# A fused Mamba-2 and mixture-of-experts layer: activation tiles of the second loop's first two steps loaded ahead of the wait for the last scatter-add, first step's norms behind the shared layer

## Chip, cores and metric

The kernel runs on one core of one Trainium2 chip. The time is that of one execution on the device, in microseconds, as the median of three runs. PE is the matmul engine (TensorE; PEld are its weight loads), DVE the vector engine, ACT the scalar engine, POOL GpSimd, SP the sync engine, which issues most of the plain DMAs. Each engine works through its own list of instructions in order; semaphores tie the lists together.

## What is computed

```python
# x: [2, 4096, 256]
x = x + layernorm(mamba2(layernorm(x)))        # attention half, the kernel's first part
h = layernorm(x)
# feed-forward half, 8192 tokens, 64 experts, 8 per token, 128 slots for each expert
gu = h @ shared_gate_up_w                       # shared layer, inner width 512
shared = silu(gu[:, :512]) * gu[:, 512:] @ shared_down_w
shared = shared * sigmoid(h @ shared_gate_w)
probs = softmax(h @ gate_w); w, idx = top_k(probs, 8)
buf[e, slot] = h[token]                         # gather per expert, capacity 128
out_e = (silu(buf @ Wg) * (buf @ Wu)) @ Wd      # per expert, inner width 128
routed = sum over the token's experts of w * out_e
x = x + layernorm(routed + shared)
```

## The kernel before, in words

The first part (Mamba-2) leaves the residual x in SBUF (x_all), the normed and transposed activations in DRAM as 32 tiles (xnt_d, one tile is 2 x 128 tokens, 256 KB), the tables of token numbers for each expert, and zeros in routed_sum in DRAM. The part at issue has two software-pipelined loops over tiles and experts. A function iteration(i) is written for each engine; it is unrolled for the first four steps and the last ones and runs as a hardware loop for the middle. real(j, n) tells whether stage j exists in this step; follows(i) is false only in the very first step, i = 0.

**First loop** (iteration_r1, 16 steps). Each step takes four of the 64 experts: POOL gathers their tokens by indirect DMA, PE multiplies, ACT and DVE make silu and product, ACT scales the result into out_e, and POOL adds it to routed_sum in DRAM by an indirect DMA that adds (scatter-add). These scatter-adds are strictly one after another: each waits for the semaphore of the one before (added00, added01, added10, added11). Beside this each step computes the shared layer of one tile (tiles 0 to 15): ACT rounds the tile to xt_hi, DVE makes the rest xt_lo = xt - xt_hi and raises xt_split, PE does the up product in three passes for each of four column groups (up_shared, 12 matmuls each of 128x256) and the down product (down_shared, 12 matmuls for each batch), and the result is kept in SBUF (shared).

**Second loop** (iteration_r2, 8 steps, two trailing stages). Each step computes the shared layer of two more tiles (16 + 2 j in xt[0], 17 + 2 j in xt[1]) and finishes four tiles: two from the first loop's stored rows (indices 1 and 3 of routed, f_sum, f_norm) and two fresh ones (indices 0 and 2). To finish a tile means: load its rows of routed_sum (routed), add the shared part (f_sum), bn_stats, bn_aggr, on POOL the variance plus epsilon and the power -0.5, on DVE the shift, on ACT the norm (f_norm), on POOL the add to x_all (f_ready), on SP the store. The tiles routed, f_sum and f_norm lie in the same SBUF as the experts' buffers (out_e among them), xt does not.

The order of the lists, for step i = j0:

- SP (L1279 to L1317): in step 0 a wait for all scatter-adds (added11 at 256, L1283); loads routed[1] (L1285), xt[0] (L1288), xt[1] (L1291), routed[3] (L1294); the stores of earlier tiles and the load of routed[2] (L1309); wait for f_ready1, its store (L1313), load of routed[0] (L1316).
- PE (L1429 on): second half of the down product of the step before; wait for m_act_split3; two down products of the step before (bank 0); wait for xt_split; eight up_shared; first half of the down product of this step.
- ACT (L1552 on): m_act_high0 and m_act_high3 of the step before; f_norm[0] of two steps before; xt_hi[0], xt_hi[1]; f_norm[2] of two steps before; four silu and copies of the first tile, with f_norm[1] after the fourth silu (L1597); those of the second tile; at the end f_norm[3] (L1625).
- DVE (L1746 on): m_act_s 3, splits 0 and 3 of the step before (L1762, L1765, raises m_act_split3); f_sum[0] of the step before; add of routed[1] (L1780); xt_lo[0] (L1783, raises xt_split); statistics of f_sum[1] (L1792, L1798); add of routed[3] (L1802); xt_lo[1] (L1805); products and splits of both tiles, with the remaining steps of the norms between them (L1812, L1824, L1834, L1877).
- POOL (L1967 on): powers and adds; for step 0 variance 1 and power 1 (L1994, L1997), add of f_norm[1] (L2001), variance 3 and power 3 (L2004, L2007), and in step 1 the add of f_norm[3] (L1982).

Of the kernel before, what the change touches and what calls it, by code (L numbers as in the profile page):

```python
# [54 lines left out]
def plain(v):  # L55

    return v.bitcast(F32)
# [7 lines left out]
def build(nc, x_d, w_in_d, conv_w_d, conv_b_d, dt_bias_d, a_log_d, d_d, norm_w_d, w_out_d,  # L65
# [7 lines left out]
    with ctx:  # L73
# [1124 lines left out]
        m_xt_high = sem("m_xt_high")  # L1198
        m_gate_ready = sem("m_gate_ready")
# [28 lines left out]
        with nc.Block() as block:  # L1228
            @block.sync
            def _(eng):  # L1230
# [47 lines left out]

                def iteration_r2(i):  # L1279
                    j0, j1, j2 = i, i - 1, i - 2  # L1280
                    if real(j0, 8):
                        if is_number(j0) and j0 == 0:
                            eng.wait_ge(added11, 256)  # L1283
                        eng.nop(nofuse=True)
                        eng.dma_start(routed[:, 1], tokens_of(routed_d[0:TOK, :], 2 * j0 + 0)).then_inc(routed_loaded1, 16)  # L1285
                    if real(j0, 8):
                        eng.nop(nofuse=True)
                        eng.dma_start(xt[:, 0].rearrange("p k t -> p (k t)"), xnt_d[bass.ds(2 * j0 + 16, 1), :, :].rearrange("o p f -> (o p) f")).then_inc(xt_loaded, 16)  # L1288
                    if real(j0, 8):
                        eng.nop(nofuse=True)  # L1290
                        eng.dma_start(xt[:, 1].rearrange("p k t -> p (k t)"), xnt_d[bass.ds(2 * j0 + 17, 1), :, :].rearrange("o p f -> (o p) f")).then_inc(m_xt_loaded, 16)  # L1291
# [174 lines left out]
            def _(eng):  # L1466
# [85 lines left out]
                def iteration_r2(i):  # L1552
# [77 lines left out]
            def _(eng):  # L1630
# [115 lines left out]
                def iteration_r2(i):  # L1746
# [42 lines left out]
                    if real(j0, 8):  # L1789
# [4 lines left out]
                    if real(j0, 8):  # L1794
# [5 lines left out]
                    if real(j0, 8):  # L1800
# [8 lines left out]
                    if real(j0, 8):  # L1809
# [10 lines left out]
                    if real(j0, 8):  # L1820
# [11 lines left out]
                    if real(j0, 8):  # L1832
# [42 lines left out]
                    if real(j0, 8):  # L1875
# [8 lines left out]
                    if real(j1, 8):  # L1884
# [4 lines left out]
                        last.then_inc(f_stats2, 1)  # L1889
                pipeline(eng, iteration_r2, 4, 8, 10)  # L1890
# [152 lines left out]
```

## Time and profile before

| | |
|---|---|
| runs | 1491.86, 1495.43, 1496.35 us |
| median | 1495.43 us |
| span of the profiled execution | 1491.0 us, from its first to its last instruction |
| its own time | not given apart; only the three times above |
| PE busy | 1259.5 us (84%) |
| DVE busy | 1054.9 us (71%) |
| ACT busy | 937.5 us (63%) |
| POOL busy | 845.2 us (57%) |
| mean granted TensorE clock | 0.947 |

A row of an engine in order of time has the start in the span, the duration, the engine, the line of the kernel, the operation, out<-in by the program's names and the shapes, and in brackets the idle time of the engine before it with what ended it. experts_arena is the SBUF region that holds xt, routed, f_sum, f_norm and the small norm tiles, counts holds silu_s and act_s, bank is PSUM. L1468 is the line of a copy helper on ACT. The clock is given as a share of full speed: 1.0 is 2.4 GHz, 0.5 is 1.2 GHz.

### The profile page before, as it was taken

The page shows a single profiled execution, that of the slowest core. Times are in us where ns is not written, and L with a number is a line of the kernel's source. Part 1 is how long each engine was busy: PE and PEld are TensorE (multiplying, and loading weights), DVE is VectorE, ACT ScalarE, POOL GpSimd, SP SyncE. Part 2 cuts the span into 40 slices and gives each one's busy share as a digit, 9 for nine tenths or more (in the row PEclk, how much of TensorE's full clock was granted, in tenths as well). Part 3 has the DMA queues.
Part 4 walks back from the last instruction along what each step waited for, and adds up shares of the span by engine and source line. Part 5 has one row for each costly group of instructions (what it writes and reads, how often), then busy time and mean ns, then how long its engine had stood idle before and what let it go on. Part 6 is the DMA issues. An engine that isn't in the chain of part 4 may idle for free. (4 is left out here: it accounts for less than half of the span.)

```text
span 1491.0 us, 27525 instructions
## 1 busy us (share of the span) xinstructions
PE 1259.5 (84%) x8578; PEld 1095.7 (73%) x8578; DVE 1054.9 (71%) x3152; ACT 937.5 (63%) x2097; POOL 845.2 (57%) x1039
## 2 busy tenths in 40 slices
PE   2898999999999999999999998268877888749995
PEld 2677787787787787787787786268777887739995
DVE  3788899899899899899899896423233333328995
ACT  2777877877877878878878876623333333325663
POOL 0365566566566565565565565156766667624554
PEclk9999999999999999999999999579899989979998
DMA  5500110010010010010010000466666666624452
GB/s 165 171 15 15 33 39 24 32 37 23 32 37 23 32 37 23 32 37 23 32 37 23 21 29 19 119 181 161 148 156 155 164 152 161 136 46 132 153 159 94
DMA packets 110628, 115.66 MB, mean 78 GB/s; under 512 B 19633, under 2 KB 98801, under 8 KB 110577
## 3 DMA queue, kind: packets, MB, share of 16 engines
q1 hardware_dynamic: 95440, 90.38, 19.3%
q0 software_dynamic: 14336, 23.08, 8.4%
q10 hardware_dynamic: 800, 1.57, 0.3%
q8 instruction: 25, 0.41, 0.1%
q14 instruction: 27, 0.21, 0.0%
HBM read 68.53 MB, written 46.47 MB: 77 GB/s over the span
## 5 line engine op out<-in xcount | busy, mean ns | idle before, releaser
L1012 POOL TENSOR_TENSOR mamba_arena<-mamba_arena 128x512 f32<-128x512 f32 (+2 forms) x384 | 383.3, 1009 | 298.9 <-DVE mamba_arena L791 201.3
L1331 PE MATMUL bank<-xt_hi,wsgu_hi 128*128 128x256 f32 x512 | 152.0, 297 | 33.7 <-DVE xt_lo L1783 19.9
L449 PE MATMUL bank<-identity,mamba_arena 128*128 128x128 f32 x704 | 112.2, 279 | 53.4 <-DVE mamba_arena L900 27.2
L1331 PE MATMUL bank<-xt_lo,wsgu_hi 128*128 128x256 f32 x512 | 147.0, 287 | 0.0
L1331 PE MATMUL bank<-xt_hi,wsgu_lo 128*128 128x256 f32 x512 | 146.9, 287 | 0.0
L791 DVE TENSOR_TENSOR mamba_arena<-bank,mamba_arena 128x512 f32<-128x512 f32 (+1 forms) x224 | 136.3, 610 | 14.6 <-PE bank L493 7.8
L449 PEld LDWEIGHTS bank<-identity,mamba_arena 128*128 128x128 f32 x704 | 84.8, 145 | 80.3 <-issue 27.0
L1331 PEld LDWEIGHTS bank<-xt_hi,wsgu_hi 128*128 128x128 f32 x512 | 100.4, 196 | 35.6 <-DVE xt_lo L1783 21.3
L657 ACT ACTIVATE mamba_arena<-bank 128x512 f32<-128x512 f32 x192 | 100.3, 539 | 6.6 <-PE bank L449 3.8
L1331 PEld LDWEIGHTS bank<-xt_lo,wsgu_hi 128*128 128x128 f32 x512 | 100.5, 196 | 0.4
L1331 PEld LDWEIGHTS bank<-xt_hi,wsgu_lo 128*128 128x128 f32 x512 | 100.2, 196 | 0.0
L791 DVE TENSOR_TENSOR mamba_arena<-mamba_arena 128x512 f32<-128x512 f32 (+1 forms) x128 | 54.7, 427 | 48.9 <-ACT mamba_arena L657 46.7
L661 ACT ACTIVATE mamba_arena<-x_all,mamba_arena 128x256 f32 (+1 forms) x128 | 70.0, 595 | 16.1 <-DVE mamba_arena L837 11.0
L791 DVE TENSOR_TENSOR mamba_arena<-bank_s,mamba_arena 128x1024 f32<-128x1024 f32 x64 | 77.8, 1216 | 2.4 <-ACT bank_s L696 2.2
L1338 PE MATMUL bank<-wsdown_hi,act_hi 128*128 128x256 f32 x256 | 78.6, 307 | 0.4 <-DVE act_lo L1765 0.4
L1338 PE MATMUL bank<-wsdown_lo,act_hi 128*128 128x256 f32 x256 | 73.5, 287 | 0.0
L1338 PE MATMUL bank<-wsdown_hi,act_lo 128*128 128x256 f32 x256 | 73.3, 286 | 0.0
L1012 POOL TENSOR_TENSOR mamba_arena<-mamba_arena,minus_half 128x2 f32<-128x2 f32 x96 | 68.2, 710 | 7.8
L589 PEld LDWEIGHTS bank<-mamba_arena 128*128 128x128 f32 x256 | 46.9, 192 | 31.1 <-ACT mamba_arena L747 17.8
L754 ACT ACTIVATE run_moving<-bank,head_of 64x128 fp32r<-64x128 f32 x256 | 68.4, 361 | 0.4
L589 PE MATMUL bank<-mamba_arena 128*128 128x256 f32 x256 | 64.4, 395 | 0.6
L471 PEld LDWEIGHTS bank<-mamba_arena 128*128 128x128 f32 x256 | 48.5, 190 | 20.0 <-issue 14.9
(354 smaller groups left out, 4324.9 us busy)
## 6 DMA issues: line engine op xcount, KB each, us to landing
experts_arena<-in_egu SPq DMA_DIRECT2D x64, 256.0 KB
routed_sum<-zeros SPq DMA_DIRECT2D x1, 8320.0 KB, 27.0
x_all<-in_x SPq DMA_DIRECT2D x32, 256.0 KB, 2.7
token_table<-mamba_arena SPq DMA_DIRECT2D x64, 128.0 KB, 1.7
normed_transposed<-mamba_arena SPq DMA_DIRECT2D x32, 256.0 KB, 2.0
experts_arena<-normed_transposed SPq DMA_DIRECT2D x32, 256.0 KB, 4.2
experts_arena<-in_edown SPq DMA_DIRECT2D x64, 128.0 KB
experts_arena<-routed_sum SPq DMA_DIRECT2D x32, 256.0 KB, 3.2
```

Of the source, the lines that this page charges most:

```text
L449: return nc.tensor.transpose(out, in_, identity[:, :])
L471: last = nc.tensor.matmul(bank[0][:, 1 * DM:2 * DM], yt[:, 1, c, :], w_out[:, c, :], start=c == 0, stop=c == KI - 1)
L589: last = nc.tensor.matmul(bank[0][:, 0 * DM:1 * DM], yt[:, 0, c, :], w_out[:, c, :], start=c == 0, stop=c == KI - 1)
L657: return nc.scalar.activation(out, in_, ACT.Copy)
L661: last = nc.scalar.activation(out[:, b, :], x[b], ACT.Identity, bias=shift[:, b:b + 1], scale=scale[:, b:b + 1])
L754: last = nc.scalar.activation(run_moving[0:HALF, h, :], bank[2][0:HALF, 0:P], ACT.Copy, scale=head_of[0:HALF, h:h + 1])
L791: return nc.vector.tensor_tensor(out, a, b, op)
L1012: return nc.gpsimd.tensor_tensor(out, a, b, op)
L1331: last = nc.tensor.matmul(out[:, f * 256:(f + 1) * 256], w[:, k, columns], x[:, k, :], start=n == 0, stop=n == len(parts) - 1)
L1338: last = nc.tensor.matmul(out[:, b * DM:(b + 1) * DM], x[:, c, b * P:(b + 1) * P], w[:, c, :], start=c + n == 0, stop=c == FS // P - 1 and ...
```

## The change

On SP the loads of xt[0] and xt[1] get a function of their own, load_tiles. In the first step of the second loop SP waits for the first loop's last tile split (xt_split at 16), loads the tiles of step 0, waits for both splits of step 0 (xt_split at 17 and a new semaphore m_xt_split, which DVE raises at xt_lo[1]), loads the tiles of step 1, and only then waits for added11 at 256. Step 1 loads none; from step 2 on each step loads its tiles ahead of routed[1]. On DVE, in step 0 alone, the eight entries of tiles 1 and 3 (adds, statistics, aggregates, shifts) stand at the end of the step; on ACT, in step 0 alone, f_norm[1] stands behind the last silu, ahead of f_norm[3]. All other steps keep their order on DVE and ACT. PE and POOL are unchanged.

```diff
@@ -1276,19 +1277,27 @@
+                def load_tiles(j):
+                    eng.nop(nofuse=True)
+                    eng.dma_start(xt[:, 0].rearrange("p k t -> p (k t)"), xnt_d[bass.ds(2 * j + 16, 1), :, :].rearrange("o p f -> (o p) f")).then_inc(xt_loaded, 16)
+                    eng.nop(nofuse=True)
+                    eng.dma_start(xt[:, 1].rearrange("p k t -> p (k t)"), xnt_d[bass.ds(2 * j + 17, 1), :, :].rearrange("o p f -> (o p) f")).then_inc(m_xt_loaded, 16)
+
                 def iteration_r2(i):
                     j0, j1, j2 = i, i - 1, i - 2
+                    if not follows(i):
+                        eng.wait_ge(xt_split, 16)
+                        load_tiles(0)
+                        eng.wait_ge(xt_split, 17)
+                        eng.wait_ge(m_xt_split, 1)
+                        load_tiles(1)
+                    if real(j0 - 2, 8) and real(j0, 8):
+                        load_tiles(j0)
                     if real(j0, 8):
                         if is_number(j0) and j0 == 0:
                             eng.wait_ge(added11, 256)
                         eng.nop(nofuse=True)
                         eng.dma_start(routed[:, 1], tokens_of(routed_d[0:TOK, :], 2 * j0 + 0)).then_inc(routed_loaded1, 16)
-                    if real(j0, 8):
-                        eng.nop(nofuse=True)
-                        eng.dma_start(xt[:, 0].rearrange("p k t -> p (k t)"), xnt_d[bass.ds(2 * j0 + 16, 1), :, :].rearrange("o p f -> (o p) f")).then_inc(xt_loaded, 16)
-                    if real(j0, 8):
-                        eng.nop(nofuse=True)
-                        eng.dma_start(xt[:, 1].rearrange("p k t -> p (k t)"), xnt_d[bass.ds(2 * j0 + 17, 1), :, :].rearrange("o p f -> (o p) f")).then_inc(m_xt_loaded, 16)
...
@@ -1591,7 +1600,7 @@
-                    if real(j0, 8):
+                    if real(j0, 8) and follows(i):
                         eng.wait_ge(f_shift1, j0 + 1)
                         for b in range(NB):
                             last = nc.scalar.activation(f_norm[:, 1, b, :], f_sum[:, 1, b, :], ACT.Identity, bias=fshift[:, 1, b:b + 1], scale=frs[:, 1, b:b + 1])
...
@@ -1619,6 +1628,11 @@
+                    if real(j0, 8) and not follows(i):
+                        eng.wait_ge(f_shift1, j0 + 1)
+                        for b in range(NB):
+                            last = nc.scalar.activation(f_norm[:, 1, b, :], f_sum[:, 1, b, :], ACT.Identity, bias=fshift[:, 1, b:b + 1], scale=frs[:, 1, b:b + 1])
+                        last.then_inc(f_normed1, 1)
                     if real(j0, 8):
                         eng.wait_ge(f_shift3, j0 + 1)
...
@@ -1775,7 +1789,7 @@
-                    if real(j0, 8):
+                    if real(j0, 8) and follows(i):
                         eng.wait_ge(routed_loaded1, 16 * j0 + 16)
                         nc.vector.tensor_tensor(f_sum[:, 1], routed[:, 1], shared[:, :, bass.ds(2 * j0 + 0, 1), :].rearrange("p b o d -> p (b o) d"), ALU.add).then_inc(f_added1, 1)
...
                     if real(j0, 8):
                         eng.wait_ge(m_xt_high, j0 + 1)
-                        nc.vector.tensor_tensor(xt_lo[1][:, :, :], xt[:, 1], plain(xt_hi[1][:, :, :]), ALU.subtract)
+                        nc.vector.tensor_tensor(xt_lo[1][:, :, :], xt[:, 1], plain(xt_hi[1][:, :, :]), ALU.subtract).then_inc(m_xt_split, 1)
...
@@ -1887,6 +1901,40 @@
+                    if real(j0, 8) and not follows(i):
+                        eng.wait_ge(routed_loaded1, 16 * j0 + 16)
+                        nc.vector.tensor_tensor(f_sum[:, 1], routed[:, 1], shared[:, :, bass.ds(2 * j0 + 0, 1), :].rearrange("p b o d -> p (b o) d"), ALU.add).then_inc(f_added1, 1)
+                    if real(j0, 8) and not follows(i):
+                        eng.wait_ge(f_added1, j0 + 1)
+                        for b in range(NB):
+                            last = nc.vector.bn_stats(fst[:, 1, b, :], f_sum[:, 1, b, :])
+                        last.then_inc(f_stats1, 1)
...
+                    if real(j0, 8) and not follows(i):
+                        eng.wait_ge(f_scale3, j0 + 1)
+                        nc.vector.scalar_tensor_tensor(fshift[:, 3, :], fmv[:, 3, :, 0], -1.0, frs[:, 3, :], ALU.mult, ALU.mult).then_inc(f_shift3, 1)
                 pipeline(eng, iteration_r2, 4, 8, 10)
```

## Rows read from the trace of the kernel before

**Rows 1.** Chain of work that ended last, 1286 us on: start us, us, what

```profile
1289.83 4.78 DMA routed_sum<-experts_arena,scatter_now
...
1298.63 0.69 POOL experts_arena L1963
...
1313.72 3.70 DMA routed_sum<-experts_arena,scatter_now
...
1322.72 3.75 DMA routed_sum<-experts_arena,scatter_now
...
1329.87 0.64 ACT xt_hi L1468
...
1331.27 14.23 PE bank L1331 x96
...
1345.91 0.98 ACT experts_arena L1625 x2
...
1348.73 3.13 PE bank L1338 x24
1351.86 11.52 PE bank L1331 x96
1363.38 5.76 PE bank L1338 x48
1369.14 11.78 PE bank L1331 x96
```

**Rows 2.** PE in order of time: start us, us, line, what, [idle before <-releaser]

```profile
1331.27 0.58 PE L1331 MATMUL bank<-xt_hi,wsgu_hi 128*128 128x256 f32 x1 [19.86 <-DVE xt_lo L1783]
```

**Rows 3.** SP's DMA issues in order of time, first loop's last, second loop's first

```profile
1292.35 0.43 SPq L1263 DMA_DIRECT2D experts_arena<-in_edown  x1
1326.53 0.38 SPq L1285 DMA_DIRECT2D experts_arena<-routed_sum  x1
```

**Rows 4.** DVE in order of time, last tile split of loop one, then step 0

```profile
1282.44 0.69 DVE L1687 TENSOR_TENSOR xt_lo<-experts_arena,xt_hi 128x512 fp32r<-128x512 f32 x1
...
1329.23 0.69 DVE L1780 TENSOR_TENSOR experts_arena<-experts_arena 128x512 f32<-128x512 f32 x1 [20.22 <-DMA experts_arena<-routed_sum]
...
1331.14 0.74 DVE L1792 BATCH_NORM_STATS2 experts_arena<-experts_arena 128x6 f32<-128x256 f32 x2
1331.98 0.25 DVE L1798 BATCH_NORM_AGGREGATE experts_arena<-experts_arena 128x2 f32<-128x6 f32 x2
```

**Rows 5.** ACT in order of time, its last act of the first loop

```profile
1311.45 0.84 ACT L1533 ACTIVATE experts_arena<-bank,experts_arena 128x256 f32<-128x256 f32 x2 [0.58 <-PE bank L1338]
```

**Rows 6.** Short windows: stretch, length, busy us (instructions) by engine, PEclk, DMA, GB/s

```profile
1316.00:1318.00 2.00, 0.00 (x0) 0.00 (x0) 0.00 (x0) 0.00 (x0) 0.00 (x0) 0.60 0.41 58
1336.00:1338.00 2.00, 2.00 (x15) 2.00 (x15) 0.78 (x4) 1.01 (x3) 0.00 (x0) 0.78 0.00 0
```

**Rows 7.** POOL in order of time, step 0, and one row of the last step

```profile
1332.73 1.06 POOL L1997 TENSOR_TENSOR experts_arena<-experts_arena,minus_half 128x2 f32<-128x2 f32 x1
1341.21 1.09 POOL L2001 TENSOR_TENSOR x_all<-x_all,experts_arena 128x512 f32<-128x512 f32 x1 [7.42 <-ACT experts_arena L1597]
...
1342.75 0.71 POOL L2007 TENSOR_TENSOR experts_arena<-experts_arena,minus_half 128x2 f32<-128x2 f32 x1
...
1480.63 0.71 POOL L1971 TENSOR_TENSOR experts_arena<-experts_arena,minus_half 128x2 f32<-128x2 f32 x1
```

**Rows 8.** ACT in order of time, norm 1 of step 0, a norm at the end

```profile
1340.05 1.09 ACT L1597 ACTIVATE experts_arena<-experts_arena 128x256 f32<-128x256 f32 x2
...
1481.57 1.09 ACT L1563 ACTIVATE experts_arena<-experts_arena 128x256 f32<-128x256 f32 x2 [7.33 <-DVE experts_arena L1759]
```

**Rows 9.** ACT in order of time, step 5, second tile

```profile
1420.25 0.63 ACT L1468 ACTIVATE xt_hi<-experts_arena 128x512 fp32r<-128x512 f32 x1 [0.76 <-DMA experts_arena<-normed_transposed]
```

**Rows 10.** DVE in order of time, step 5, add of routed[1]

```profile
1420.38 0.68 DVE L1780 TENSOR_TENSOR experts_arena<-experts_arena 128x512 f32<-128x512 f32 x1
```

**Rows 11.** Waits of 1350 to 1470 us: who for whom, us, times, longest

```profile
PEld bank L1331 <- DVE xt_lo L1783: 1.2, 6, 0.2
```

More of the change, by code:

```diff
@@ L1198, in build @@
         m_xt_high = sem("m_xt_high")
+        m_xt_split = sem("m_xt_split")
         m_gate_ready = sem("m_gate_ready")
@@ L1788, in iteration_r2 @@
                         nc.vector.tensor_scalar(gate_s[:, 1, :], of_step(shared_tanh, 2 * j1 + 17), 1.0, 0.5, ALU.add, ALU.mult).then_inc(m_gate_ready, 1)
-                    if real(j0, 8):
+                    if real(j0, 8) and follows(i):
                         eng.wait_ge(f_added1, j0 + 1)
@@ L1793, in iteration_r2 @@
                         last.then_inc(f_stats1, 1)
-                    if real(j0, 8):
+                    if real(j0, 8) and follows(i):
                         eng.wait_ge(f_stats1, j0 + 1)
@@ L1799, in iteration_r2 @@
                         last.then_inc(f_mean1, 1)
-                    if real(j0, 8):
+                    if real(j0, 8) and follows(i):
                         eng.wait_ge(routed_loaded3, 16 * j0 + 16)
@@ L1808, in iteration_r2 @@
                         nc.vector.tensor_tensor(act_s[:, 0, 0], bank[2][:, NB * P:2 * NB * P], silu_s[:, 0, 0], ALU.mult).then_inc(act_ready0, 1)
-                    if real(j0, 8):
+                    if real(j0, 8) and follows(i):
                         eng.wait_ge(f_added3, j0 + 1)
@@ L1819, in iteration_r2 @@
                         nc.vector.tensor_tensor(act_lo[0][:, 0], act_s[:, 0, 0], plain(act_hi[0][:, 0]), ALU.subtract).then_inc(act_split0, 1)
-                    if real(j0, 8):
+                    if real(j0, 8) and follows(i):
                         eng.wait_ge(f_stats3, j0 + 1)
@@ L1831, in iteration_r2 @@
                         last.then_inc(f_stats0, 1)
-                    if real(j0, 8):
+                    if real(j0, 8) and follows(i):
                         eng.wait_ge(f_scale1, j0 + 1)
@@ L1874, in iteration_r2 @@
                         last.then_inc(f_mean0, 1)
-                    if real(j0, 8):
+                    if real(j0, 8) and follows(i):
                         eng.wait_ge(f_scale3, j0 + 1)
@@ new lines, in iteration_r2 @@
+                    if real(j0, 8) and not follows(i):
+                        eng.wait_ge(f_stats1, j0 + 1)
+                        eng.nop(nofuse=True)
+                        for b in range(NB):
+                            last = nc.vector.bn_aggr(fmv[:, 1, b, :], fst[:, 1, b, :])
+                        last.then_inc(f_mean1, 1)
+                    if real(j0, 8) and not follows(i):
+                        eng.wait_ge(routed_loaded3, 16 * j0 + 16)
+                        nc.vector.tensor_tensor(f_sum[:, 3], routed[:, 3], shared[:, :, bass.ds(2 * j0 + 1, 1), :].rearrange("p b o d -> p (b o) d"), ALU.add).then_inc(f_added3, 1)
@@ new lines, in iteration_r2 @@
+                    if real(j0, 8) and not follows(i):
+                        eng.wait_ge(f_added3, j0 + 1)
+                        for b in range(NB):
+                            last = nc.vector.bn_stats(fst[:, 3, b, :], f_sum[:, 3, b, :])
+                        last.then_inc(f_stats3, 1)
+                    if real(j0, 8) and not follows(i):
+                        eng.wait_ge(f_stats3, j0 + 1)
+                        eng.nop(nofuse=True)
+                        for b in range(NB):
+                            last = nc.vector.bn_aggr(fmv[:, 3, b, :], fst[:, 3, b, :])
+                        last
@@ new lines, in iteration_r2 @@
+                    if real(j0, 8) and not follows(i):
+                        eng.wait_ge(f_scale1, j0 + 1)
+                        nc.vector.scalar_tensor_tensor(fshift[:, 1, :], fmv[:, 1, :, 0], -1.0, frs[:, 1, :], ALU.mult, ALU.mult).then_inc(f_shift1, 1)
+                    if real(j0, 8) and not follows(i):
+                        eng.wait_ge(f_scale3, j0 + 1)
+                        nc.vector.scalar_tensor_tensor(fshift[:, 3, :], fmv[:, 3, :, 0], -1.0, frs[:, 3, :], ALU.mult, ALU.mult).then_inc(f_shift3, 1)
```

## The prediction

> **What bounds the kernel now.** The page's busy shares are averages over two loops with different limits, so I read them only to see that PE (TensorE) is the busiest engine, and then took the chain of work that ended last from 1286 us on, the engines in order of time around the seam between the two loops, and short windows for clock and DMA. The chain [rows 1] is, up to 1326.5 us, a string of scatter-adds into routed_sum, each waiting for the one before; then loads, then PE without a break nearly to the end. Between them lies the seam: PE stands idle for 19.9 us, from 1311.4 to 1331.27 [rows 2]. The scatter-adds need neither PE nor the second loop's activation tiles.
>
> Behind the seam the chain is PE alone: 96 up matmuls in 11.5 to 11.8 us and 48 down matmuls in 5.76 us a step [rows 1]. So a microsecond taken out of the seam reaches the end, if nothing else in it is late.
>
> **Part 1: the tile loads go ahead of the wait.** SP issued its last expert load at 1292.35 and then stood until 1326.53 [rows 3]. xt[0] was read last by the split of tile 15 (1282.44, 0.69 us) [rows 4], and xt[1] is unused in the first loop. So both tiles of step 0 are issued at about 1292.9 and lie there long before ACT is ready. ACT works in order: its last act of the first loop (shared rows of step 15) runs 1311.45 to 1312.3 [rows 5]. From the start of xt_hi to PE's first matmul it took 1.40 us (1329.87 to 1331.27) [rows 1]; the moved add no longer stands ahead of xt_lo on VectorE (DVE), whose first instruction of the loop is now the split. PE starts step 0 at about 1313.6, 17.7 us earlier.
>
> Without routed_sum it can do the 96 up matmuls (11.6 us) and the first down product of both batches (24 matmuls, 2.9 us); it then reaches the wait for m_act_split3 at about 1328.2. The granted clock fell 5 us after PE's last matmul (window 1316 to 1318: 0.60) [rows 6], so a start after 2.2 us of idling is at full clock.
>
> **Part 2: what is late next.** m_act_split3 is made at the head of step 1 by ACT and DVE, and ahead of it on ACT stand the two norms of step 0, which need routed_sum and so the wait for the last scatter-add. The gain of part 1 ends there. With the norms in their old place DVE would stand at the first add before act_s of step 0; moved behind the shared layer, they are the only work left when the scatter-adds end. From there:
> - routed[1] is issued at 1326.53 and used by DVE at 1329.23, as before [rows 3, 4]; routed[3] follows it directly.
> - Add 0.69, then 0.10 until a dependent instruction starts (statistics at 1331.14 last 0.74, the aggregate starts at 1331.98) [rows 4]: statistics 1330.0, aggregate 1330.9. POOL's (GpSimd's) power ended 1.81 after the aggregate's start (1333.79 less 1331.98) [rows 4, 7]: 1332.7. Meanwhile DVE does second add, statistics and aggregate (0.8, 0.8, 0.2) to 1332.8. So shift 1 at 1332.8, ACT's norm 1 at 1333.0.
> - POOL's residual add starts 1.16 after the norm (1340.05 to 1341.21), its second power 1.54 after that (to 1342.75), and a norm 0.94 after the power's start (1480.63 to 1481.57) [rows 7, 8]: norm 3 at 1336.65.
> - From norm 3 to PE's next matmul 2.82 (1345.91 to 1348.73) [rows 1]: 1339.5.
>
> Before, that matmul started at 1348.73 [rows 1]. Gross gain 9.2 us.
>
> **Part 3: the clock.** PE now idles from 1328.2 to 1339.5, 11.3 us. Before, the clock fell to half (1.2 GHz) in the seam and came back to full (2.4 GHz) 5.5 us after the restart (window 1336 to 1338: 0.78) [rows 6]. That restart made 96 matmuls take 14.23 us, against 11.52 and 11.78 later: 2.45 to 2.7 dearer [rows 1]. The old restart now costs nothing, since it isn't there, but neither did step 0's speed matter to 1339.5; a new one is paid on the path at 1339.5, mostly in the 24 down matmuls (3.1 us before, about 5 now). I take 2.6, bounds 0 (clock kept) and 4. Net 6.6.
>
> The Trainium skill (TensorE: Matmul & The Clock Gate, What's actually happening) says that the activity monitor runs free of the kernel, so that the point of the change of clock varies from run to run. By that the price would lie somewhat under or over that of the one restart read here; the sum doesn't use it.
>
> **Part 4: what the early loads collide with.** The tiles of step 1 are issued when both splits of step 0 are done, about 1314.4. One scatter-add is under way (1313.72, 3.70 us), and the later ones stand in line behind it [rows 1]. Such a transfer took 3.70 and 3.75 us in the quiet tail and 4.78 beside expert loads (1289.83) [rows 1]. So 0 to 1.1 us; I take 0.9, since the two overlap wholly, and it contains what DVE, ACT and PE at work beside the last three may add. The step 0 tiles share with the scatter-add ahead of 1298.63, where the chain runs over POOL's gathers and not over the transfer [rows 1]: 0. The last experts' rows may come up to 1 us later; that only moves PE's early start, which has 11 us to spare.
>
> The Trainium skill (DMA: Bandwidth & Descriptors, Queues, rings and completion order) speaks against this part: a DMA engine takes turns between the rows that have work, so a tile load takes its share from a scatter-add under way. By that rule the transfer could take up to twice its time while the tiles last, and this term would be larger than 0.9.
>
> **Part 5: steps 1 to 7.** Step 1: routed[0] and routed[1] are issued right behind f_ready1 (1335.3, the add's start at 1334.2 and its 1.09 us [rows 7]) and are wanted by DVE at about 1339.4 and 1340.3; with no tile in that burst and 2.70 us from issue to use on a quiet ring [rows 3, 4] they are in time. DVE's order from m_act_split3 to xt_lo is the old one, PE didn't wait there before (1348.73 and 3.13 make 1351.86) [rows 1], and its down matmuls take 2 us longer at half clock. From step 2 on the two tiles go ahead of routed[1], which moves from third to fifth place in a burst of six 256 KB transfers. In step 5 ACT waited 0.76 us for the tile in fifth place and had it at 1420.25 [rows 9]; DVE takes routed[1] at 1420.38 [rows 10], and PE already waits 0.2 us a step for the split behind it (1.2 us, 6 times) [rows 11]. The cover is 0.13 us there; what routed[1] is late beyond it goes one to one onto the step. Value 0, bounds 0 and 0.8 a step (one place, by ACT's wait). The added increment of m_xt_split and SP's wait for it (reached at 1314.3; behind it stand only load_tiles(1) and the old wait for added11) cost nothing.
>
> **The sum.** 9.2 - 2.6 - 0.9 = 5.7 us: span 1491.0 to 1485.3. The profiled execution's own time isn't given apart from its span; the median of the three runs, 1495.43, lies 4.4 us over that span, which I keep: **1489.7 us**.
>
> **Rivals.**
> - Clock kept through 11 us of idling: 9.2 - 0.9 = 8.3, 1487.1. Against: it fell after 5 us before [rows 6]. 0.07.
> - Scatter chain dragged: the last three transfers take 4.78 instead of 3.75 each, 3.1 instead of 0.9: 3.5 saved, 1491.9. For: the pace beside a working loop. Against: no tile is left after about 1318. 0.12.
> - routed[1] late by half a place beyond its cover, 0.4 in six steps: 5.7 - 2.4 = 3.3, 1492.1. 0.10.
> - **Slower**: at the same point routed[1] loses both places that it gives up, 1.6 less 0.13, in steps 2 to 7: 8.8 lost against 5.7 won, 1498.5. It turns slower from 1.1 us of lateness a step. Against: the fifth place was in time by ACT's row. 0.04.
> - It doesn't do what it says: something holds step 0 until the scatters end all the same, 1495.4. Against: neither ACT nor DVE has work from 1312.3 to 1329. 0.05.
> - Forecast: 0.62, own range 1488.2 to 1491.2.
>
> **How the numbers follow.** A measurement of this kernel tells 0.3% (4.5 us) from no change; the limit is 1490.9, close above the forecast. Of the forecast's 0.62 about 0.50 lies under it, with 0.07 from the kept clock and 0.02 from the scatter rival: faster 0.59. Slower 0.05, same 0.36. The range, 1485.8 to 1494.3, goes from the kept clock less 1.3 of the runs' spread to the dragged scatter together with the late routed[1]; outside it lie the slower and the nothing-gained rivals and the tails of the others, 0.2.
>
> **What would show it.** Right: up matmuls of step 0 at 1313 to 1315 with the clock at 1.0; a new PE idle stretch of 10 to 12 us that ends with down matmuls at 1339 to 1341; clock 0.5 before it and for about 5 us after. Wrong: scatter-adds that end after 1328 (part 4), DVE idle for routed_sum in steps 2 to 7 (part 5), norm 3 later than 1338 (part 2), or the 24 down matmuls in 3 us (part 3).

## The result, and the profile after

Over 13 runs of each, the changed kernel has a median of 1488.89 us and the kernel before one of 1495.19 us. The ratio is 0.9965 with a 95% interval of 0.995 to 0.998, so 0.35% (5.2 us) faster, with 3.0 to 7.5 us inside the interval. The forecast was 1489.7 us. The profiled execution of the changed kernel took 1485.44 us, its span is 1483.7 us.

The seam between the loops, as the chain of work that ended last in the changed kernel shows it (start us, us, what):

```profile
1312.12 4.56 DMA routed_sum<-experts_arena,scatter_now
1317.46 3.79 DMA routed_sum<-experts_arena,scatter_now
1322.00 3.78 DMA routed_sum<-experts_arena,scatter_now
1325.84 2.89 DMA experts_arena<-routed_sum
...
1332.38 1.10 ACT experts_arena L1634 x2
1333.56 1.09 POOL x_all L2049
1334.91 0.72 POOL experts_arena L2055
1335.85 1.09 ACT experts_arena L1639 x2
1337.28 1.11 DVE act_lo L1776
1338.78 5.49 PE bank L1347 x24
1344.27 11.66 PE bank L1340 x96
```

From the first load of routed rows to the down matmuls it is 12.94 us (1325.84 to 1338.78); before it was 22.20 (1326.53 to 1348.73, [rows 1, 3]). PE's 96 up matmuls of step 0, which stood between, are gone from the chain. They answer to [rows 2] in PE's own order of time (start us, us, engine, line, what, [idle before <-releaser]):

```profile
1311.50 0.39 PE L1340 MATMUL bank<-xt_hi,wsgu_hi 128*128 128x256 f32 x1 [2.17 <-DVE xt_lo L1797]
...
1338.78 0.58 PE L1347 MATMUL bank<-wsdown_hi,act_hi 128*128 128x256 f32 x1 [12.62 <-DVE act_lo L1779]
```

SP's issues, as [rows 3]: the tiles of step 0, those of step 1, then the first routed load.

```profile
1287.91 0.38 SPq L1282 DMA_DIRECT2D experts_arena<-normed_transposed  x1
...
1312.10 0.33 SPq L1282 DMA_DIRECT2D experts_arena<-normed_transposed  x1
1312.48 0.43 SPq L1284 DMA_DIRECT2D experts_arena<-normed_transposed  x1
1325.84 0.38 SPq L1300 DMA_DIRECT2D experts_arena<-routed_sum  x1
```

And short windows of the changed kernel, as [rows 6] (stretch, length, busy us and instructions of PE, PEld, DVE, ACT, POOL, granted clock, DMA share, GB/s):

```profile
1312.00:1314.00 2.00, 2.00 (x20) 2.00 (x19) 0.39 (x2) 0.38 (x1) 1.55 (x1) 1.00 0.38 103
...
1326.00:1328.00 2.00, 0.16 (x2) 0.00 (x0) 0.00 (x0) 0.00 (x0) 0.00 (x0) 1.00 0.35 120
...
1330.00:1332.00 2.00, 0.00 (x0) 0.00 (x0) 1.81 (x6) 0.00 (x0) 1.15 (x2) 0.71 0.00 0
...
1342.00:1344.00 2.00, 2.00 (x11) 2.00 (x11) 1.28 (x4) 0.00 (x0) 1.50 (x2) 0.50 0.00 0
1344.00:1346.00 2.00, 2.00 (x17) 2.00 (x16) 0.00 (x0) 0.11 (x1) 0.00 (x0) 0.88 0.00 0
```

In this trace step 0 runs at full clock (1.00). PE then idles 12.6 us, in which the clock falls to 0.50 (1.2 GHz), and the down matmuls pay for it.

**How two traces are compared here.** The whole gain is a third of a per cent, and the first loop alone wanders by as much. Number the 64 scatter-adds 0 to 63; interval 58, say, is the time from the start of scatter-add 58 to that of 59. Number 56 starts ahead of anything that the change touches, at 1289.83 before and at 1285.59 after. Those 4.2 us are chance; a second trace of the changed kernel, taken with the experiments, has 1290.90. So each trace is cut in three: up to scatter-add 56; from there to the first routed load, 36.70 us before and 40.25 after (the **scatter chain**); and from that load to the end, 164.47 before and 157.86 after (the **tail**). The 7.3 us between the spans are 4.24 of chance, less 3.55, plus 6.61.

### The profile page after: what moved, and what is told of

Same layout as the page of the kernel before. It is cut to its first block and busy times, and to the rows that moved or that the text cites. A ratio compares the mean times of both kernels' runs of the same rounds, so it can differ in the third digit from the quotient of the medians.

```text
span 1483.7 us, 27527 instructions
## 1 busy us (share of the span) xinstructions
PE 1261.0 (85%) x8578; PEld 1097.0 (74%) x8578; DVE 1054.3 (71%) x3152; ACT 936.4 (63%) x2097; POOL 845.8 (57%) x1039
## 5 line engine op out<-in xcount | busy, mean ns | idle before, releaser
L1347 PE MATMUL bank<-wsdown_hi,act_hi 128*128 128x256 f32 x256 | 79.4, 310 | 12.6 <-DVE act_lo L1779 12.6
```

Of the source, the lines that this page charges most:

```text
L1347: last = nc.tensor.matmul(out[:, b * DM:(b + 1) * DM], x[:, c, b * P:(b + 1) * P], w[:, c, :], start=c + n == 0, stop=c == FS // P - 1 and ...
```

## The experiments

The ratio and its interval are each against the kernel before on the same chip. Two kernels were first profiled once more unchanged, for the size of the wander.

**The kernel before, again.**

> The kernel before, unchanged, a second trace. It shows how far a trace wanders by itself: the stretch from the first routed load of the second loop to the end should again be 164.5 within 0.7 us, while the time of that load wanders by some us. Whether the scatter-adds of 1289 to 1306 took 5.57 and 4.64 us in the first trace by their nature (then again) or by chance (then 0.5 to 1.5 more, as in the kernels with and without early tiles) is open.

Scatter chain 37.94, tail 163.27 (first trace 36.70 and 164.47). The restart at half clock cost less this time, since the clock was back sooner, 3.0 us after the restart (granted clock 0.93 from 1336 to 1338) against 5.6 us in the first trace (0.78 in [rows 6]):

```profile
1333.29 13.08 PE bank L1331 x96
```

**The changed kernel, again.**

> The changed kernel, unchanged, a second trace: the stretch from the first routed load to the end should again be 157.9 within 0.7 us, the clock half for about 5.5 us from the restart near the first load plus 13, and the scatter-add beside the tiles of step 1 0.8 to 1.1 us longer than its neighbours.

Scatter chain 41.41, tail 157.69, and 12.89 us from the routed load to the down matmuls. Chain of work:

```profile
1322.54 4.99 DMA routed_sum<-experts_arena,scatter_now
...
1332.31 2.85 DMA experts_arena<-routed_sum
...
1345.20 5.49 PE bank L1347 x24
```

The tail reproduces to 0.2 us. The scatter chain is the part that varies, and it was longer than before in both traces of the changed kernel. One thing didn't reproduce: step 0 again started after 2.17 us of idling (1314.82 to 1317.00), but here at half clock. Windows:

```profile
1316.00:1318.00 2.00, 1.00 (x4) 1.00 (x5) 1.29 (x2) 0.74 (x2) 1.27 (x1) 0.73 0.00 0
1318.00:1320.00 2.00, 2.00 (x12) 2.00 (x11) 0.00 (x0) 0.04 (x1) 0.37 (x1) 0.50 0.63 150
```

Nothing on the path paid for it, since PE still had 12.1 us to idle behind step 0.

**Only the tiles early.** The kernel before, with SP's loads of step 0's tiles ahead of its wait; the norms stay in their old place.

```diff
...
+                    if not follows(i):
+                        eng.wait_ge(xt_split, 16)
+                        load_tiles(0)
...
-                    if real(j0, 8):
-                        eng.nop(nofuse=True)
...
+                    if real(j0, 8) and follows(i):
+                        load_tiles(j0)
...
```

> The kernel before, with the two tiles of step 0 issued ahead of the wait for the last scatter-add; the norms stay where they were and the tiles of step 1 are not early. My theory (the early tiles are worth little alone, because VectorE still stands at the add of routed[1] ahead of the split): xt_lo follows the add directly, so PE starts step 0 at 0.60 + 0.74 us after the add's start instead of 2.04 us, 0.7 us earlier; time 0.5 to 1 us under the kernel before, not to be told from it, about 1494.5. Rival (the tile transfers are what the seam waited for): PE's start moves by 10 us or more and the time falls by the full 6 us of the change.

Median 1492.63, ratio 0.9995 (0.9982 to 1.0009): no change that can be told. Chain of work:

```profile
1328.61 2.87 DMA experts_arena<-routed_sum
...
1331.50 0.69 DVE experts_arena L1785
...
1332.85 13.61 PE bank L1336 x96
```

PE starts 4.24 us after the routed load, against 4.74 before (1326.53 to 1331.27). With the tile long there, DVE's first instruction is still the add that needs routed_sum, and xt_lo stands behind it. The early load alone is worth 0.5 us there.

**Only the norms late.** The changed kernel with SP's list put back as it was before.

```diff
...
-                    if not follows(i):
-                        eng.wait_ge(xt_split, 16)
-                        load_tiles(0)
-                        eng.wait_ge(xt_split, 17)
-                        eng.wait_ge(m_xt_split, 1)
-                        load_tiles(1)
...
```

> The changed kernel with SP's old order: all tiles behind the wait for the last scatter-add; only the norms of step 0 are moved behind the shared layer. My theory (the place of the norms pays only together with the early tiles): PE starts step 0 as in the kernel before, runs its 96 up and 24 down matmuls, and then waits for adds, statistics and both norms, which take some 10 us from the first add (read from the changed kernel: 1328.75 to 1338.78) instead of 0.6 us of idling there, so the step 1 down matmuls start 5 to 7 us later than before, and the clock falls on top for up to 2.4: 6 to 9 us slower than the kernel before, 1501 to 1504. Rival (the norms behind the layer are by themselves a gain or free, since they leave VectorE to the layer first): within 2 us of the kernel before or faster.

Median 1502.72, ratio 1.0057 (1.0036 to 1.0078): slower. Chain of work:

```profile
1333.99 12.64 PE bank L1331 x84
...
1351.35 1.10 ACT experts_arena L1625 x2
...
1354.82 1.09 ACT experts_arena L1630 x2
...
1357.75 5.49 PE bank L1338 x24
```

The shared layer and the norms now stand one behind the other after the wait, and the tail is 172.87. Neither half of the change brings anything alone: one is worth 0.5 us, the other costs 8 to 10, together they take 5.4 to 6.8 us out of the tail.

**Step 1's tiles not early.** The changed kernel, with load_tiles(1) in step 1.

```diff
-                        eng.wait_ge(xt_split, 17)
-                        eng.wait_ge(m_xt_split, 1)
-                        load_tiles(1)
-                    if real(j0 - 2, 8) and real(j0, 8):
+                    if real(j0 - 1, 8) and real(j0, 8):
```

> The changed kernel without the early load of step 1's tiles: they are loaded in step 1, ahead of routed[1]; step 0's are early as in the change. My theory (these two transfers do nothing but slow one scatter-add, 4.56 against 3.8 us, since step 1's tiles are wanted only at 1340): the scatter-add during which they ran takes 3.8 us again, the last one ends 0.8 us earlier relative to its neighbours, PE does not wait for the split of step 1, and the time is 0.5 to 1 us under the changed kernel. Rival (step 1's tiles have to be early): behind f_ready1 they share a burst with the store and three routed loads, ACT gets the first one at about 1339 to 1340 and the split ends after 1344.3, so PE waits and the time is 1 us or more above the changed kernel. The transfer of the scatter-add of 1296.64, 5.55 us in the changed kernel against 3.85 before, has the step 0 tiles in both; if they caused it, it is above 5 us here and in the first experiment too, if not, it is about 3.8 in some.

Median 1486.81, ratio 0.9945 (0.9926 to 0.9965), tail 157.86, to the hundredth that of the changed kernel. DVE waited 1.39 us for routed[1] in step 1 and PE didn't notice, since its down matmuls ran at half clock. The early load of step 1's tiles brings nothing by itself. Without it interval 61 was 4.84 us, against 5.34 and 5.81 in the two traces of the changed kernel; the 0.5 to 1 us that I expected of this isn't resolved by the times, whose intervals overlap. The question about scatter-add 58 is answered: its interval was 6.41 here and 4.68 with only the tiles early, and it was 5.90 with only the norms late, where no tile is early at all. So the tiles of step 0 aren't its cause.

**The clock kept up.** The changed kernel with 84 more matmuls in PE's idle stretch, ahead of the wait for m_act_split3. Nothing reads their product.

```diff
+                    if is_number(i) and i == 1:
+                        for _ in range(7):
+                            down_shared(bank[5], 0, 0)
```

> The changed kernel with 84 matmuls added on PE whose product nobody reads (seven down products into an unused PSUM bank), between the first down product of step 0 and the wait for m_act_split3; the kernel's own result is complete. They fill 10.1 of PE's 12.6 us of idling. My theory (the stall costs its length and, on top, a restart at half clock): the granted clock stays at 1.0 through the stall, the 24 down matmuls behind it take 2.9 to 3.1 us instead of 5.49, and the time is 2.2 to 2.7 us under the changed kernel, about 1486.4. Rival (PE at half clock hides behind something else in step 1): the down matmuls are fast but PE then waits by as much at the first up matmul or at the bank of f_added0, and the time is unchanged.

Median 1485.65, ratio 0.9951 (0.9936 to 0.9967). Its window and its chain:

```profile
1342.00:1344.00 2.00, 0.48 (x4) 0.48 (x5) 1.84 (x4) 1.33 (x3) 0.84 (x1) 1.00 0.94 313
```

```profile
1343.52 3.14 PE bank L1347 x24
1346.66 11.52 PE bank L1340 x96
```

The 24 matmuls take 3.14 us instead of 5.49, and the tail is 155.11, 2.6 to 2.75 less than in the two traces of the changed kernel. That is the price of the restart. The executions as a whole don't resolve it: the intervals overlap.

**The clock kept up, step 1's tiles late.** The last two edits together.

> The changed kernel with both of the edits tried singly before: step 1's tiles loaded in step 1, and 84 unread matmuls in PE's stall. If the two are independent, the scatter-add in which the tiles of step 1 were carried takes 3.8 us (0.8 to 1 less), the granted clock stays at 1.0, and the time is 3.2 to 3.7 us under the changed kernel, about 1485.4. The rival for the late tiles (PE, now at full clock, reaches the up matmuls of step 1 2.4 us earlier and the tile is not there yet): in the third experiment the first up matmul followed the down products at once with 5.49 us of cover; with 3.1 us of down products it waits 0.5 us or more for xt_lo and the gain is under 2.5 us.

Median 1486.8, ratio 0.9938 (0.992 to 0.9955), tail 156.13: 1.7 under the changed kernel, 1.0 over the kernel with the clock alone. DVE and PE in step 1:

```profile
1352.83 0.70 DVE L1794 TENSOR_TENSOR experts_arena<-experts_arena 128x512 f32<-128x512 f32 x1 [1.49 <-DMA experts_arena<-routed_sum]
...
1354.19 0.39 PE L1337 MATMUL bank<-xt_hi,wsgu_hi 128*128 128x256 f32 x1 [0.76 <-DVE xt_lo L1797]
```

With the tiles back in step 1's burst, routed[1] is 1.49 us late for DVE, and at full clock 0.76 of it reaches PE. So the early load of step 1's tiles has a worth only once the clock price is gone.

**routed[1] first again.** The changed kernel, with load_tiles(j0) behind routed[1] from step 2 on.

> The changed kernel with SP's old order from step 2 on: routed[1] ahead of the two tiles. My theory (routed[1] in fifth place is in time but for one step): the single wait of VectorE for routed_sum in step 5 (0.2 us) and PE's extra 0.3 us there are gone, everything else is the same, time within 0.5 us of the changed kernel. Rival (the place costs PE in every step, hidden in the pipeline): the steps from step 2 on, 17.4 to 17.8 us apart, come closer together by 0.1 us or more each and the time falls by 1 us or more.

Median 1488.14, ratio 0.9956 (0.9938 to 0.9974), tail 157.21. In the first trace of the changed kernel step 5 is the one step that is longer than its neighbours. Its chain there:

```profile
1396.74 6.03 PE bank L1340 x48
...
1408.84 4.20 DMA experts_arena<-routed_sum
...
1414.54 11.77 PE bank L1340 x96
```

and the same steps with routed[1] first:

```profile
1399.24 11.78 PE bank L1340 x96
...
1416.78 11.77 PE bank L1340 x96
```

17.80 us (1396.74 to 1414.54) against 17.54: the 0.26 are the late routed[1]. That putting it first removes them isn't shown by this one trace, because the second trace of the changed kernel doesn't have them either (its steps are 17.52 to 17.54 apart). What all traces together say is weaker: none of the five with routed[1] ahead of the tiles has a step over 17.54 from step 2 on, and of the nine others two have one that is 0.26 longer and three some that are 0.1 to 0.2 longer. The rest by which this tail is shorter than the changed kernel's lies mostly at the seam (12.69 us from the load to the down matmuls, which then took 5.34).

**One step further.** After the experiments with the clock the idle stretch was the thing left to fill. Here step 1's up matmuls no longer stand behind step 0's norms: ACT and DVE make step 1's act_hi, act_lo, xt_hi and xt_lo at the end of step 0, and SP loads step 0's routed rows in the order 0, 1, 3, 2. PE waits only for the rows that its bank holds up.

```diff
...
+                        if is_number(i) and i == 1:
+                            eng.wait_ge(f_added0, 1)
...
+                    if not follows(i):
+                        eng.wait_ge(m_act_ready0, 1)
+                        copy(act_hi[1][:, 0], act_s[:, 1, 0]).then_inc(m_act_high0, 1)
...
+                        copy(xt_hi[1][:, :, :], xt[:, 1]).then_inc(m_xt_high, 1)
...
```

> The changed kernel with more of the layer ahead of step 0's norms. On ACT and VectorE the makers of m_act_split3 and of both tile splits of step 1, and the add of routed[0], stand ahead of the adds and norms of step 0; SP loads routed[0], [1], [3], [2] of step 0 first and routed[1], [3] of step 1 as soon as the adds of step 0 have read theirs; PE waits for f_added0 before it writes bank 1 in step 1. My theory (the stall of 12.6 us that is left exists only because the norms stand ahead of these on ACT and VectorE, and costs its length and 2.6 us of clock): PE runs on after the first down product with 24 down and 48 up matmuls (8.7 us) and then waits for act_ready0 of step 1, which comes behind the norms, at about 2.5 us after where norm 3 starts now; its idle time is 3 to 5 us in place of 12.6 and the clock stays at 1.0; the stretch from the first routed load to the end, 157.9 us in the changed kernel, becomes 146 to 149, and the time 1478 to 1480. Rival (what is moved only comes late elsewhere: VectorE, busy over nine tenths in the loop, has to make up for the norms in step 1): step 1 grows by 3 us or more over its 17.5 and the gain over the changed kernel is 8 us or less.

Median 1481.34, ratio 0.9906 (0.9887 to 0.9925), tail 151.75: it beats both kernels, by 6.1 us of tail over the changed one. PE's idle stretch is short now (PE in order of time, then two windows):

```profile
1344.45 0.58 PE L1357 MATMUL bank<-xt_hi,wsgu_hi 128*128 128x256 f32 x1 [2.65 <-DVE counts L1854]
```

```profile
1342.00:1344.00 2.00, 0.00 (x0) 0.00 (x0) 1.90 (x6) 0.89 (x3) 1.57 (x2) 1.00 0.00 2
1344.00:1346.00 2.00, 1.55 (x7) 1.55 (x8) 2.00 (x9) 1.00 (x3) 0.85 (x2) 0.55 0.39 131
```

I had expected a tail of 146 to 149. The 2.65 us of idling, and the clock at 0.55 behind it, took part of that. The clock fell 2.4 us after PE's last matmul here (1341.80), far sooner than in the seam before (5.0).

**And its norms spread.** The kernel just shown, with shift 3, norms 1 and 3 and the statistics of step 1 moved in between the products, to close the 2.65 us.

> The kernel with the layer ahead of the norms, changed once more: in step 1 VectorE makes the first products of the tile before shift 3 of step 0 and the statistics of step 1, and ACT's norms 1 and 3 of step 0 and norm 1 of step 1 stand between the silus, so that neither engine stands still for POOL's 3.3 us (add and power) between the two shifts. My theory (of the gain that was expected there, 9 to 12 us, the missing 3 to 6 went into PE's idle stretch of 2.7 us from 1341.7 and the half clock behind it, because act_ready0 of step 1 stood behind that wait): PE has no idle stretch over 2 us between the loops' seam and the last step, the clock stays at 1.0, and the stretch from the first routed load to the end is 147 to 149 us in place of 151.75; time 1477 to 1479. Rival (VectorE is full: the work of two steps' norms in step 1 comes out somewhere): PE's waits reappear at the head of step 2 or in it, and the gain over the kernel before it is under 1.5 us.

Median 1483.41, ratio 0.994 (0.9922 to 0.9959), tail 151.07. The clock stays at 1.00 through 1348, but who waits for whom shows a longer wait of PE, now ahead of a down product (us, times, longest):

```profile
PE bank L1364 <- DVE counts L1974: 5.7, 1, 5.7
```

One hole was exchanged for another, for 0.7 us of tail, where 3 to 5 were expected. The times don't show even that: this ratio is 0.994 and that of the kernel just shown 0.9906.

**Program code moved.** In many traces one scatter-add interval, number 58, was about a microsecond or more longer than its neighbours, with a packet of program code under way in it (last section). Two kernels were to move only the place of the program's code: the changed kernel with 100 empty instructions ahead of the feed-forward part, on PE alone, and on the other four engines alone.

> The changed kernel with 100 empty instructions on PE alone, ahead of its feed-forward part, far from the seam; nothing else differs. In seven traces of kernels with the norms behind the shared layer the third last-but-three scatter-add interval (number 58 of 0 to 63) was 5.85 to 6.41 us, and in each a single 16 KB packet of the instruction queue was under way in it, 2.2 to 3.5 us after its start; elsewhere it was 4.64 to 4.72. Theory (a packet of program code delays one DMA engine's part of the scatter-add): if the code is PE's, the packet moves to another time, interval 58 falls to 4.6 to 4.8, and the interval that gets the packet, if one does, may take 5.4 or more. If the code is another engine's, the packet and the 5.9 to 6.4 stay where they are. Rival (the interval is long for another reason, such as the order of the second loop or chance): 58 stays at 5.9 to 6.4 though the packet has gone, or falls though the packet is still there. Tail from the first load of routed rows to the end as before, 157.7 to 157.9.

> The changed kernel with 100 empty instructions on each of SP, ACT, DVE and POOL, ahead of their feed-forward parts, none on PE. Theory (program code): if the packet in interval 58 is the code of one of these four, it moves, and interval 58 falls to 4.6 to 4.8 us from 5.85 to 6.41. Of this run and the one with PE's padding exactly one should move that packet, or this one moves others as well. Rival: 58 stays at 5.9 to 6.4 without a packet, or falls with one. Tail 157.7 to 157.9.

Interval 58 was 5.36 and 5.84 us, and in both the packet was still in it (2.3 and 3.0 us after its start). Neither kernel moved it, so they don't tell whose code it is. What the packet does is read from the DMA queues in the last section. Their tails are 156.36 and 157.54; the first has a cheaper restart:

```profile
1342.11 4.44 PE bank L1349 x24
```

## Why the prediction was right

**Part 1, right.** PE started step 0 at 1311.50, 14.3 us ahead of the first routed load, at full clock. This trace was 4 us ahead at scatter-add 56, so the position against the load is what counts: forecast 12.9 (1313.6 against 1326.5). One sentence of it holds less often than I thought: that a start after 2.2 us of idling is at full clock. It was so in eight of the ten traces with both an early step 0 and the late norms. In two, the second of the changed kernel and the one of the kernel that goes a step further, the clock had fallen some 2 us into the idling, and step 0 ran its first 3.3 us at half clock. It cost nothing, for the reason that part 3 of the forecast gives: the speed of step 0 doesn't matter until the norms are done.

**Part 2, right.** From the routed load to the down matmuls 13.0 was forecast and 12.94, 12.89 measured; norm 3 came 10.0 us after the load (forecast 10.1). The step that carries it: the norms are what is late next, and their length could be put together from rows of the kernel before. The kernels with half of the change each bear it out, one with 0.5 us won and one with a longer tail.

**Part 3, right.** 2.6 was forecast for the clock. Keeping the clock up was worth 2.6 to 2.75 in the tail. The fall came some 4.7 us into the idling (0.71 in the window from 1330 to 1332), much as in [rows 6]. The price of one restart varies more than I allowed for the value taken: with the norms late the 24 matmuls took 5.49 in five traces, 5.34 in one and 4.44 in another, against 3.14 at full clock, and with the old order the 96 took 14.23, 13.61 and 13.08 against 11.52, so 1.3 to 2.7 us. It goes with how long the clock stays at half behind the restart: 3.0 us where the price was 1.3 and 1.6 (4.44 and 13.08), 5.6 and 5.7 where it was 2.7 and 2.5 (14.23, and 5.49 with 11.66). The Trainium skill (TensorE: Matmul & The Clock Gate, What's actually happening) says that the monitor runs free of the kernel and that the point of the change varies; these traces agree, with that spread.

Parts 2 and 3 together made 9.2 less 2.6, a tail shorter by 6.6. The two traces of each kernel give 5.4 to 6.8, 6.1 in the mean.

**Part 4, the term that was too small.** I took 0.9 for the scatter chain. In the two traces of the changed kernel it was longer by 3.5 (40.25 and 41.41 against 36.70 and 37.94). By interval, mean of two against mean of two, 1.6 of that is interval 58, 1.0 is 61, 0.6 is 62 and 0.4 is 56; the rest are alike. So the collision that I priced, the tiles of step 1 beside one scatter-add (61), cost 1.0 here, and the load of step 0's tiles beside 56 cost nothing that can be told (5.44 to 6.63 with it, 5.57 to 6.06 without). What the term lacked are the packets of program code behind which parts of scatter-adds 58 and 62 stood; the part had put nothing down for them. Over all traces it is 36.7 to 38.7 where no tile load is early (three traces, mean 37.8) and 37.3 to 41.4 where both are (eight, mean 39.5), so 1.7 on average, not 0.9, with as much wander. These are not eight traces of one kernel: of the three, one has the norms late and interval 58 long, and of the eight, the two that go a step further have it short. More on both causes below. The two traces alone would give a gain of 2.6 us (6.1 less 3.5), which lies outside the interval of the 13 runs (3.0 to 7.5); with the average 1.7 it is 4.4, inside it. The rival of the dragged chain (3.1) had its size partly right, but not its mechanism: the last three transfers took 4.56, 3.79 and 3.78 us and not 4.78 each; single ones were hit.

**Part 5, right.** The value was 0. In one trace of the changed kernel the cover of 0.13 us failed in one step of six, by 0.26 us, and in the other in none. The rivals of a late routed[1] in each step, the slower one among them, fell.

**The other rivals.** The clock wasn't kept, and the change does what it says.

The sum said 5.7. The medians differ by 6.3, the ratio says 5.2. The agreement is closer than the parts deserve and partly luck, since part 4 alone was off by 0.8 on average and by 2.6 in the two pairs of traces. The runs of whole executions confirm the sum, with 3.0 to 7.5 us inside their interval; they can't confirm its parts.

## What to carry to other kernels

Where two lists of work wait for the same late event, moving one ahead of it pays only if the other stops standing in front of it: cost the two edits together, since each half alone here was worth 0.5 us or cost 8. Read the new gain from the chain that is late next, put together from rows of the old trace, and charge the new idle stretch of PE with one restart of the clock (1.3 to 2.7 us here). When the gain is a third of a per cent, cut the traces at an event ahead of the change and compare the parts, because the chance in the first 1290 us is as large as the effect.

## What the runs showed that I had not expected

**When a tile load hits a scatter-add.** The load of step 1's tiles (512 KB) falls beside scatter-add 61. What it costs goes with the time between the two issues. Eight traces, interval from scatter-add 61 to 62:

| tiles issued after scatter-add 61 by | interval, us |
|---|---|
| -0.02, 0.33, 0.81, 0.88 | 5.34, 5.65, 6.14, 5.81 |
| 1.41, 1.41 | 4.96, 4.90 |
| 1.69, 2.87 | 4.58, 4.56 |
| no tile there (six traces) | 4.48 to 4.84 |

So the collision costs 0.7 to 1.5 us when the loads are issued within 0.9 us of the scatter-add, 0.3 at 1.4 us, and nothing from 1.7 us on. In none of the eight was a packet of program code under way in that interval. The Trainium skill (DMA: Bandwidth & Descriptors, Queues, rings and completion order) says that a DMA engine takes turns between the rows that have work. The trace agrees for loads issued early, where the transfer took 4.56 against 3.79 us; the loads that came 1.7 us later took no time from it that can be seen. My 0.9 lies inside the first case and leaves the second out.

**Packets of program code in the chain.** Interval 58, in code that the change doesn't touch, was 4.64 and 4.67 in the two traces of the kernel before, 4.68 with only the tiles early, and 4.64 and 4.72 in the two kernels that go a step further. In all nine others it was 5.36 to 6.41; all nine have the norms behind the shared layer, and so do the two that go a step further. POOL in the changed kernel, scatter-adds 58 and 59:

```profile
1296.64 1.62 POOL L1955 DMA_INDIRECT routed_sum<-experts_arena,scatter_now  x1 [0.52 <-issue]
1302.98 1.57 POOL L1971 DMA_INDIRECT routed_sum<-experts_arena,scatter_now  x1 [4.71 <-DMA routed_sum<-experts_arena,scatter_now]
```

The DMA queues from 1300.0 to 1301.5 show one packet of program code beside the scatter's last nine packets. First their busy share in 40 slices of that stretch, each packet counted where it starts, then the queues (queue, kind: packets, MB, share of 16 engines):

```profile
DMA  2209000000000000000000000020201000000000
...
q8 instruction: 1, 0.02, 3.7%
q0 software_dynamic: 9, 0.00, 2.8%
```

The 9 is the packet of code: it starts at 1300.11 and takes 0.90 us (3.7% of 16 engines in 1.5 us). The three small ones at the right are the scatter's last packets, of 144. They start 4.35, 4.43 and 4.51 us after the scatter-add, just when the packet of code is done; with neither such a packet nor a tile load beside it the last of the 144 starts at 3.3 to 3.7. In the second trace of the changed kernel the packet of code starts at 1303.91 and takes 1.75 us, and nine of the scatter's packets, one sixteenth of them, start one behind the other from its end on. Below are the row of 1303.8 to 1306.8 there and that of 1303.2 to 1304.7 in the kernel before, where the packet of code (the second 9, from 1303.34) is still under way when the scatter's last packet starts, and none waits for its end:

```profile
DMA  9979669579988642000000001111011010000000
```

```profile
DMA  7979301010000000000000000000000000000000
```

So the order of the packets shows what happens in a long interval: the last packets of the scatter-add start only when the packet of code is through. In eight of the nine long intervals 58, in interval 59 with only the tiles early (5.49 us), and in the three long intervals 62, the next of the late packets, one to nine in number, starts within 0.03 us of the end of the packet of code; in the kernel with the padding on PE (5.36 us) it doesn't stand out. With one to four late packets the interval grows by about 0.7 us more than these packets are late, and that rest is unexplained.

Other such packets took up to 1.8 us. A second one falls in interval 62, the last, in nine of the ten traces where step 0 starts early with the norms behind it, and in none of the other four. There the interval goes with the packet's time after the issue: 0.4 us, 4.42 to 4.54; 1.4 and 1.5 us, 4.90 and 4.93; 2.1 to 2.3 us, 5.47 to 5.89; 3.3 us, 4.63. In intervals 58 to 62 of all fourteen traces none that has neither a tile load nor such a packet beside it is over 4.84 us.

The time alone doesn't decide. The kernel before had a packet in interval 58 in both traces, 3.3 and 3.5 us after the issue, at 4.64 and 4.67 us; the changed kernel had one at 3.5 and took 6.34. With routed[1] first, packets at 3.3 us in intervals 58 and 62 of one trace went with 6.15 and 4.63. Presumably it matters whether the DMA engine that gets the code still has some of the scatter's packets; the traces don't number the engines, so this isn't shown. Whose code it is, and why interval 58 was hit in both traces of the changed kernel and in neither of the one before, stays open: the two kernels that were to move the packet didn't.
